# Zero fills of the expert regions issued in the first stages, and a product with zeros added to each slot of the second attention

## What is computed

```python
h = _L0_tok_ref(...)                                   # (8, 256, 256)
h = _layernorm(h + _L0_attn_ref(h, ...))               # causal, 8 heads of 32: "X0" in the kernel
h = _layernorm(h + _L0_ffn_ref(h, ...))                # 32 heads of 8 ("X1"), then experts with gelu
h = _layernorm(h + _L1_attn_ref(h, ...))               # gated linear attention
h = _layernorm(h + _L1_ffn_ref(h, ...))                # softmax gate, top 2 of 8 experts

# the second attention, in _L0_ffn_ref
att = jnp.einsum('bqhd,bkhd->bhqk', q, k) / np.float32(np.sqrt(hd))
p = jax.nn.softmax(att, axis=-1)
o = jnp.einsum('bhqk,bkhd->bqhd', p, v).reshape(B, S, D) @ wo + x

# the routed experts, in _L1_ffn_ref
topk_scores, topk_idx = jax.lax.top_k(gate_scores, TOP_K)
top_probs = jax.nn.softmax(topk_scores, axis=-1)
out = jnp.sum(jnp.take_along_axis(expert_out, topk_idx[..., None], axis=2) * top_probs[..., None], axis=2)
```

## Time and profile before

| | us |
|---|---|
| three timed runs | 1359.0, 1360.0, 1363.2 (median 1360.0) |
| the profiled execution | 1354.6 |
| its span | 1352.5 |
| PE, DVE, ACT, POOL busy in it | 1054.0, 735.4, 480.1, 210.0 |
| mean granted clock of PE | 0.856 of 2.4 GHz |

### The profile page before, as it was taken

How to read it: one execution, slowest core, us unless ns; L and a number is a source line. 1 busy time by engine, 2 the same in 40 slices (tenths; PEclk the granted TensorE clock), 3 DMA queues, 4 the chain that set the end, 5 groups by cost and what they waited for, 6 DMA issues and landing times. The chain is left out here.

```text
span 1352.5 us, 23102 instructions
## 1 busy us (share of the span) xinstructions
PE 1054.0 (78%) x8372; PEld 765.9 (57%) x8372; DVE 735.4 (54%) x2007; ACT 480.1 (35%) x970; POOL 210.0 (16%) x248
## 2 busy tenths in 40 slices
PE   1229968987998988989937989886636999999980
PEld 1225645443655355755524654563425999999970
DVE  7972444665535767638647656344452444444436
ACT  2111423444454443344523555251202333333322
POOL 3960000000000000200000200002013333333320
PEclk7657987988999988789977899697667999999995
DMA  5031020027422585023575130023911111111105
GB/s 162 17 73 32 1 72 18 7 76 124 52 71 101 224 162 64 33 71 106 239 126 64 64 102 1 1 63 137 376 63 40 36 37 40 37 36 40 37 28 186
DMA packets 73420, 108.88 MB, mean 81 GB/s; under 512 B 16592, under 2 KB 58336, under 8 KB 72864
## 3 DMA queue, kind: packets, MB, share of 16 engines
q1 hardware_dynamic: 66192, 74.75, 22.3%
q0 software_dynamic: 5280, 14.57, 3.3%
q10 hardware_dynamic: 1840, 18.10, 3.3%
HBM read 83.47 MB, written 40.97 MB: 92 GB/s over the span
## 5 line engine op out<-in xcount | busy, mean ns | idle before, releaser
L1658 DVE TENSOR_REDUCE mx<-scores_ps 128x4 f32<-128x1024 f32 (+1 forms) x160 | 187.0, 1169 | 143.2 <-PE scores_ps L1130 93.3
L1491 ACT ACTIVATE pt<-turned_ps 128x1024 f32<-128x1024 f32 (+1 forms) x160 | 157.9, 987 | 159.9 <-PE turned_ps L1152 110.8
L2175 PEld LDWEIGHTS x_ps<-x_xtT,x_w1s 128*128 128x128 f32 x1248 | 147.2, 194 | 3.6 <-ACT x_xtT L2203 1.6
L2175 PE MATMUL x_ps<-x_xtT,x_w1s 128*128 128x128 f32 x1248 | 147.8, 277 | 1.0 <-ACT x_xtT L2203 1.0
L2189 PE MATMUL x_ps<-x_experts,x_hT 128*128 x624 | 141.0, 379 | 0.0
L2189 PEld LDWEIGHTS x_ps<-x_experts,x_hT 128*128 128x128 f32 x624 | 115.6, 190 | 14.1
L1049 POOL COPY vpad<-v 128x64 f32<-128x64 f32 x64 | 13.2, 236 | 657.9 <-PE ps L1191 543.4
L1142 PE MATMUL turned_ps<-q,k 32*128 32x256 f32 x512 | 70.7, 353 | 48.2 <-DVE mx L1658 20.0
L1142 PEld LDWEIGHTS turned_ps<-q,k 32*128 32x128 f32 x512 | 43.2, 202 | 105.5 <-issue 44.7
L2218 ACT ACTIVATE x_hT<-x_ps,x_b1c 128x128 f32<-128x128 f32 x312 | 84.9, 382 | 16.9 <-issue 13.8
L2237 DVE COPY x_w1s<-x_experts 128x2048 f32 x39 | 56.1, 1441 | 51.0 <-PE x_ps L2175 39.3
(11 more groups left out here) (423 smaller groups left out, 1947.7 us busy)
## 6 DMA issues: line engine op xcount, KB each, us to landing
x_slots<-x_slots ACTq DMA_DIRECT2D x4, 4160.0 KB
wexp<-in_L_ffn_w SPq DMA_DIRECT2D x16, 1024.0 KB, 5.3
x_experts<-in_L_ffn_W SPq DMA_DIRECT2D x16, 1024.0 KB, 13.5
q<-heads SPq DMA_DIRECT2D x48, 128.0 KB, 5.3
k<-heads SPq DMA_DIRECT2D x48, 128.0 KB, 10.3
ha<-h SPq DMA_DIRECT2D x16, 256.0 KB, 3.2
x_pair<-y_rows SPq DMA_DIRECT2D x4, 1024.0 KB, 9.1
heads<-nat_k_hi SPq DMA_DIRECT2D x12, 256.0 KB, 4.0
```

The costliest lines, as they stand in the source:

```text
L1491: sc.activation(pt[v.index // 2 % (PT_RING // 2)][:, :, 0:wide], turned_ps[:, :, 0:wide], ACT.Exp)\
L1658: v.tensor_reduce(mx[:, u.group % 2, 0:blocks, u.n:u.n + 2].rearrange("p b n -> p n b"), scores_ps[:, :, 0:blocks * (P if u.causal else T) ...
L2175: last = mm(ps[2 * (i % 2) + f // KH][:, f % KH * P:(f % KH + 1) * P], w1s[:, i % 2, c, f * P:(f + 1) * P], xtT[:, i % 2, c, :], start=c = ...
```

## The change

The four copies are issued by a function of their own, `zero_rows`, one ahead of each of the second to the fifth stage of stream a (Y3 of pair 1, Y2 and Y2s of pair 0, Y3 of pair 2). `scatter` waits for all four in pair 0 and for none later. And each X1 slot with transposed scores adds one product to the bank of its first unit, between the scores and `add_maxima`: `identb` by the first column of `mask_s`, which is zero throughout, repeated over 512 columns.

```diff
@@ scatter, in the block of gpsimd
-            if p < PAIRS // 2:
-                pool.wait_ge(sg("zeros"), 32 * (p + 1))
+            if p == 0:
+                pool.wait_ge(sg("zeros"), 16 * PAIRS)
@@ x_slot, in the block of tensor
+            if vs and not vs[0].causal:
+                mm(ps[2 + vs[0].index % 2][:, :], identb[:, :], mask_s[:, 0:1].to_broadcast([P, 2 * T]), start=False,
+                   stop=False, skip_group_check=True)
             for v in vs:
                 add_maxima(v)
@@ y1b, in the block of scalar
-            if p < PAIRS // 2:
-                for q in range(2 * p, 2 * p + 2):
-                    act.dma_start(xs[0:REGIONS, :].rearrange("(e q r) d -> q e r d", e=gt.E, q=PAIRS)[q],
-                                  xs[REGIONS:REGIONS + B * T // PAIRS, :].unsqueeze(0)
-                                  .to_broadcast([gt.E, B * T // PAIRS, gt.DX])).then_inc(sg("zeros"), 16)
             turned("h2", p, side)
@@ the streams of scalar
+        def zero_rows(q):
+            act.dma_start(xs[0:REGIONS, :].rearrange("(e q r) d -> q e r d", e=gt.E, q=PAIRS)[q],
+                          xs[REGIONS:REGIONS + B * T // PAIRS, :].unsqueeze(0)
+                          .to_broadcast([gt.E, B * T // PAIRS, gt.DX])).then_inc(sg("zeros"), 16)
+
         def a_stream():
-            for stage, p in plan.ORDER["a"]:
+            for n, (stage, p) in enumerate(plan.ORDER["a"]):
+                if 1 <= n <= PAIRS:
+                    zero_rows(n - 1)
                 yield from {"Y3": y3, "Y2": y2, "Y2d": y2, "Y2s": y2s, "Y1b": y1b}[stage](p)
```

## The result

The changed kernel takes 1425.4 us (median of 4 runs, 1420.7 to 1428.2) beside 1361.4 us of the kernel before (4 runs): a ratio of 1.0472, interval 1.0440 to 1.0504, **64 us slower**. The forecast was 1351 with a range to 1371; both its sign and its size are wrong. The profiled execution has a span of 1418.7 us at a mean clock of 0.876.

A forecast was written before the change was run, and what follows sets the result against it. PE, with its fixed instruction order, was taken to set the pace in the main loop. From a median of 1360.0 us, -17.7 - 2 + 1 + 27 - 17 = -8.7 us gave about 1351, range 1331 to 1371.

The forecast's parts named there:

- The copies, -17.7 - 2 + 1 = -18.7: Moved copies: PE's wait for k from heads goes (-17.7 us), clock behind it (-2), load of ha near 260 us (+1).
- The 2 us for the clock behind the wait: Just behind PE's wait for k, until 717 us: 2 us saved by the higher clock, ends 0 and 3.7.
- Rival (4): The wait for k isn't the copies'; stores of pair 3 are slow of themselves: 1369 us, chance 0.03.
- (3): Moved copies only move their harm, to the load of ha at 234 us or instruction fetches: +10, 1360 us, chance 0.1.
- "Their weight load is hidden there; here too": Second attention's 128 slots: added product's weight load is hidden, 0.22 us each at 2.4 GHz; +27 us, ends 20 and 33.
- The clock, -17, ends 0 and -36: Second attention: added products keep half of 83 us reachable at 1.2 GHz at 2.4 GHz instead; -17 us.
- "A product more doesn't leave PE idler": Reason given for the clock term's end of 0 in the second attention: the added product would return nothing.
- 6 us off for such waits: Second attention: PE's other waits, 70.4 of 614 us, absorb 6 us of the added products' cost.
- the prediction's two terms: Second attention: added products' cost, +27 us, and clock time given back, -17 us.
- The sum: Whole kernel: -17.7 - 2 + 1 + 27 - 17 = -8.7 us, about 1351 us as a median.
- Rival (1): Second attention: the clock does not answer to the added products, cost +30; +11 us in all, 1371, slower, chance 0.24.

The follow-up runs named there:

- copies_only: The changed kernel without the added products, so only the four copies of zeros moved; ratio 0.9870 to the kernel before.
- copies_again: Repeat of the moved copies without any added product, on one chip with the repeated change; ratio 0.9882 to the kernel before.
- change_again: Repeat of the full change as it is, on one chip with the repeated moved copies; ratio 1.0446 to the kernel before.
- rows32: The changed kernel with the added product on 32 rows of the array instead of 128, same 512 columns; ratio 1.0163 to the kernel before.
- two_rows: The changed kernel with two products on 32 rows each, one per unit of the slot, instead of one on all rows; ratio 1.0155 to the kernel before.
- cols128: The changed kernel with the added product over 128 columns instead of 512, all 128 rows; ratio 1.0363 to the kernel before.
- double: The changed kernel with the added product issued twice in each slot; ratio 1.0440 to the kernel before.
- behind_again: Repeat of the changed kernel with the added product behind the two maxima products instead of ahead of them; ratio 0.9995 to the kernel before.
- small_packets: The kernel before, copies in their old place, their source one zero row repeated (descriptors of 1040 bytes); ratio 1.0713 to the kernel before.
- packets_4k: The kernel before, copies in their old place, their source a block of four zero rows repeated (4160-byte packets); ratio 0.9929 to the kernel before.

## Why the prediction was wrong, step by step

- **The copies, -17.7 - 2 + 1 = -18.7.** Right: copies_only gives -17.5 and copies_again -16.1. The 2 us for the clock behind the wait can't be told apart from the measurement. Rival (4), that the wait isn't the copies', falls, and so does (3). (The other waits that the prediction sums to 49.7 and 20.7 us add up to 49.9 and 21.2 in the list; nothing hangs on it.)
- **"Their weight load is hidden there; here too": +27, ends 20 and 33.** This step failed. The price of 0.22 us was read from mask products, whose next neighbour L1202 is a product on 128 rows too (its row says 128*128). The added one stands between products on 32 rows, where its load is not hidden, nor that of the maxima products behind it. It costs 0.52 us a slot, 66.6 us in all, twice the upper end. The same product behind the maxima costs 0.23, about the 0.22 predicted.
- **The clock, -17, ends 0 and -36.** Wrong in sign. "A product more doesn't leave PE idler" excluded a loss. PE did not become idler (idle 171 us in the main loop of copies_again, 152 in change_again), and still the main loop has 38 to 68 us more at 1.2 GHz than with the copies alone (302 and 264, 329 and 261). At 0.85 of PE busy and half speed that is an estimated 16 to 29 us of cost.
- **What the parts make together.** The main loops of copies_again and change_again, on one chip (length, busy us and instructions of PE, PEld, DVE, ACT, POOL, clock, DMA share, GB/s):

```profile
96.00:1022.00 926.00, 754.78 (x5378) 484.06 (x5378) 497.02 (x1362) 354.84 (x569) 47.88 (x104) 0.86 0.34 91
96.00:1099.00 1003.00, 851.50 (x5506) 518.14 (x5506) 498.19 (x1361) 355.96 (x569) 48.11 (x104) 0.83 0.31 84
```

PE is busy 97 us more: 66.6 from the slots, and the 30 left over are near the 29 of the clock. It is idle 20 us less, 13 of them waits for DVE's maxima (28.2 and 15.6 us), so the loop grows by 77, as the ratio says (0.0564 x 1363 = 77). The prediction took 6 us off for such waits. For copies_only and after, which ran on different occasions, 66.6 + 16 = 83 would fit the 82 us between their ratios, but by luck: between those two profiled executions PE is busy 94 us more and idle 21 less, and the loop grows by 73.

- **The model in a place where it holds.** Behind the maxima the slots cost 128 x 0.22 = 28 us, and 28 to 41 us less at 1.2 GHz give an estimated 12 to 18 back: +10 to +16, beside the +10 of the prediction's two terms and +15 measured in both comparisons (0.0109 and 0.0113). In the two profiled executions on one chip the loops differ by 5 us only (926 and 931), as that of copies_again was the second slowest of its six; so the agreement is good to some 10 us. Both terms were reasonable for a product on all rows among its like.
- **The sum.** With the slots at 66.6, the rest of PE's growth at +30 and 20 off for idle time, in place of 27 and -17, it is -18.7 + 77 = +58; measured +61 in change_again and +64 in the result.
- **Rival (1)**, +11 and "slower", had the right sign, but put the cost at 30 and the clock at nothing lost. Neither rival asked what the new instruction does to its neighbours.

**Open.** Why the time at 1.2 GHz rises with products in the change's place (by 38 to 74 us over the copies alone, in rows32, two_rows, cols128 and the change), and falls with two on all rows there (double), with one ahead of the scores or with one behind the maxima. Busy time doesn't order the cases: in the main loops of change_again and behind_again PE is busy 0.85 and 0.82 of the time. One profiled execution each doesn't settle it, and two of the same kernel differ by up to 27 us.

## What to carry to other kernels

Read the price of an added matmul from a row whose neighbours on both sides take the same rows of the array as those at the new place; one on all rows between products on 32 rows costs its columns plus the overlap on both sides of it, here 0.30 us each time. On a path that PE bounds, filler pays only if it costs less than the clock gives back: here 28 us of filler behind the maxima returned an estimated 12 to 18. A large copy from one queue belongs where no small transfers that somebody waits for are issued; cut into packets of 1040 bytes it did more harm at the engine that issues it, and at 4160 bytes half of the old harm stayed.

## What the runs showed of the hardware that was not expected

- Two copies of 4160 KB in packets of 1040 bytes hold ACT at the issue for 57 and 65 us, in packets of 4160 bytes for 8.5 and 2.1 us, in large ones (53248 bytes) for 1.9 and 1.3 us. The rate falls too: 217 GB/s beside the large packets, 207 beside those of 4160 bytes, 59 beside those of 1040 bytes, in the stretches below (small_packets, then packets_4k). PE stands still in the first of them.

```profile
440.00:485.00 45.00, 0.00 (x0) 0.00 (x0) 4.21 (x18) 0.00 (x0) 0.00 (x0) 0.50 0.36 59
...
437.00:467.00 30.00, 27.85 (x152) 11.35 (x152) 22.30 (x61) 16.25 (x30) 0.41 (x2) 0.93 0.56 207
```

- The mean clock of a whole execution misleads: after has 0.876 and before 0.856, though after has more time at 1.2 GHz in its main loop. The head (0 to 96 us, PE busy 20 of them) runs at a mean of 0.63 in before and 1.00 in after, at the same length. The first row is of before, the second of after:

```profile
0.00:96.00 96.00, 20.18 (x1044) 17.78 (x1044) 84.87 (x196) 17.38 (x33) 63.80 (x66) 0.63 0.32 81
```

```profile
0.00:96.00 96.00, 21.66 (x1044) 18.63 (x1044) 84.83 (x196) 17.37 (x33) 63.83 (x66) 1.00 0.31 81
```

- The same kernel took between 1351 and 1366 us in the four series, a spread of 15 us, nearly the whole gain of the copies (16 to 17.5); so a difference of 1% was read from ratios to the kernel before, run beside on the same chip.
